# An attention and mixture-of-experts layer: each routed expert's weights loaded in two halves, the second one tile behind the first

## The reference

```python
logits = flat @ router_w.T
scores = jnp.sqrt(jax.nn.softplus(logits))
_, idx = jax.lax.top_k(scores + expert_bias, K)          # K = 4
topv = jnp.take_along_axis(scores, idx, axis=1)
topv = topv / (topv.sum(axis=-1, keepdims=True) + 1e-20)
probs = jnp.zeros((T, E), flat.dtype).at[jnp.arange(T)[:, None], idx].set(topv)

def body(acc, xs):
    wg, wu, wd, p = xs
    return (acc + p[:, None] * _clamped_swiglu(flat, wg, wu, wd), None)
out, _ = jax.lax.scan(body, jnp.zeros_like(flat), (gate_w, up_w, down_w, probs.T))
out = out + _clamped_swiglu(flat, shared_gate_w, shared_up_w, shared_down_w)
```

## Time and profile before

| | us |
|---|---|
| median of 3 runs | 1499.61 |
| lowest, highest | 1496.22, 1509.61 |
| the profiled execution's own time | 1504.55 |
| its span on the core | 1502.6 |

### The profile page before, as it was taken

How to read it: one execution, slowest core, us unless ns; L and a number is a source line. 1 busy time by engine, 2 the same in 40 slices (tenths; PEclk the granted TensorE clock), 3 DMA queues, 4 the chain that set the end, 5 groups by cost and what they waited for, 6 DMA issues and landing times.

```text
span 1502.6 us, 28760 instructions
## 1 busy us (share of the span) xinstructions
PE 1300.7 (87%) x7954; PEld 647.3 (43%) x7955; DVE 989.5 (66%) x1847; ACT 794.2 (53%) x1022; POOL 871.5 (58%) x883
## 2 busy tenths in 40 slices
PE   7999678887888888888887588799999899999998
PEld 3333234443444444444444344344444444444443
DVE  7555699999999999999999257433333233323333
ACT  2222499998999999999999431122222121212221
POOL 3111388889899999999999403434343443444441
PEclk9999699999999999999999689999999999999999
DMA  9664178776676776676777365465666666665432
GB/s 267 159 157 98 32 130 142 135 141 133 140 146 142 141 144 133 139 141 139 145 137 131 103 247 183 158 180 112 190 186 188 190 151 162 158 179 123 83 57 72
DMA packets 387509, 217.60 MB, mean 145 GB/s; under 512 B 348279, under 2 KB 348407, under 8 KB 383234
## 3 DMA queue, kind: packets, MB, share of 16 engines
q1 hardware_dynamic: 369586, 182.34, 50.0%
q0 software_dynamic: 17872, 34.64, 12.5%
HBM read 104.47 MB, written 37.49 MB: 94 GB/s over the span
## 4 chain that ended last, share of the span: by engine, by line
PE 29%; issue 21%; DMA 17%; DVE 14%; POOL 10%; ACT 5%; SPq 2%; DVEq 2%; POOLq 1%; ACTq 0%
PE psS L773 14%; DMA out_y<-mem 11%; POOL mem L649 6%; DVE mem L565 4%; DVE mem L581 4%; PE psS L781 4%; DMA mem<-mem 3%; ACT mem L526 2%; PE psS L1608 2%; PE psS L446 2%; DMA mem<-xn_dram,mem 2%; POOL mem L638 1%; DVEq L1192 1%; PE psP L765 1%; PE psP L1589 1%
## 5 line engine op out<-in xcount | busy, mean ns | idle before, releaser
L526 ACT ACTIVATE mem<-mem 128x2048 uint8<-128x2048 f32 x256 | 535.3, 2093 | 46.0 <-POOL mem L638 41.2
L649 POOL TENSOR_SCALAR mem<-mem 128x2048 bf16<-128x2048 uint8 x256 | 486.2, 1899 | 28.3 <-DMA mem<-mem 9.2
L446 PE MATMUL psS<-mem 128*128 128x512 bf16 x1024 | 312.6, 388 | 97.8 <-DVE mem L565 49.1
L773 PE MATMUL psS<-mem 128*128 (+1 forms) x752 | 356.9, 617 | 0.1
L581 DVE TENSOR_SCALAR_CACHE_REDUCE mem<-psS,mem 128x1024 f32<-128x1024 f32 x256 | 328.1, 1282 | 0.9 <-PE psS L446 0.9
L565 DVE TENSOR_SCALAR_CACHE_REDUCE mem<-psS 128x1024 f32<-128x1024 f32 x256 | 313.0, 1223 | 15.0 <-PE psS L446 11.4
L807 DVE TENSOR_SCALAR mem<-psS 128x512 f32<-128x512 f32 x94 | 65.2, 693 | 344.3 <-PE psS L773 341.3
L1170 POOL DMA_INDIRECT out_y<-mem x78 | 124.0, 1589 | 189.3 <-DMA out_y<-mem 153.0
L801 ACT ACTIVATE mem<-mem 128x256 f32<-128x256 f32 x94 | 39.4, 419 | 360.8 <-DVE mem L807 360.8
L773 PEld LDWEIGHTS psS<-mem 128*128 128x128 f32 x752 | 139.9, 196 | 151.7 <-issue 148.8
L781 PE MATMUL psS<-mem 128*128 (+1 forms) x376 | 177.1, 592 | 1.0 <-ACT mem L795 1.0
(11 more groups left out here) (213 smaller groups left out, 1192.8 us busy)
## 6 DMA issues: line engine op xcount, KB each, us to landing
mem<-in_moe_w SPq DMA_DIRECT2D x33, 1536.0 KB, 8.1
xn_dram<-mem SPq DMA_DIRECT2D x33, 256.0 KB, 2.4
mem<-in_x SPq DMA_DIRECT2D x32, 256.0 KB, 3.1
mem<-xn_dram SPq DMA_DIRECT2D x32, 256.0 KB, 3.0
out_y<-mem SPq DMA_DIRECT2D x32, 256.0 KB, 2.3
mem<-mem SPq DMA_TRANSPOSE x288, 3.1
mem<-in_ctx_in SPq DMA_DIRECT2D x16, 256.0 KB, 3.2
mem<-out_y SPq DMA_DIRECT2D x16, 256.0 KB, 4.1
```

Source lines behind the costliest of these rows:

```text
L446: last = nc.tensor.matmul(psS[c][:, k * D:(k + 1) * D], qT[pm][:, hm, :], kT[:, hm, c * HALF + k * D:c * HALF + (k + 1) * D], start=True, ...
L526: nc.scalar.activation(p8[slot], S[slot], ACT.Exp, bias=NB[:, slot:slot + 1], scale=sq[p][:, h:h + 1], accum_out=Z[p][:, h:h + 1]).then_in ...
L649: nc.gpsimd.tensor_scalar(pb[slot], pT[slot].bitcast(U8).rearrange("p (j q b) -> p j b q", b=2, q=P), 1.0, 0.0, ALU.mult, ALU.add).then_in ...
L773: last = nc.tensor.matmul(bankG[o], xT[o if xo is None else xo][:, c, :], w(c * 2 * I, 2 * I), start=(c == 0), stop=(c == DC - 1))
```

## The change

The load of an expert becomes two DMAs. Each takes half of the words of every partition row: 6 KB from each of 128 rows instead of 12 KB, 768 KB in all instead of 1,536. Where the place is free from the start (experts 0 to 7), the two are issued one behind the other. In the ring (experts 8 to 31), the first half is issued when the old load was, and the second when PE has finished one more down product, so one tile later. `expert_in` counts to 32 instead of 16 per use of a place.

```diff
+        def load_expert(sp, e, s, piece):
+            words = slice(piece * EW // 2, (piece + 1) * EW // 2)
+            sp.dma_start(ring[:, s * EW + words.start:s * EW + words.stop], moe_w[e, :, words]).then_inc(expert_in[s], 16)
+
...
                 if k < FREE_RING:
-                    sp.dma_start(ring[:, k * EW:(k + 1) * EW], moe_w[k, :, :]).then_inc(expert_in[k], 16)
+                    for piece in range(2):
+                        load_expert(sp, k, k, piece)
...
             for s in range(FREE_RING, RING):
-                sp.dma_start(ring[:, s * EW:(s + 1) * EW], moe_w[s, :, :]).then_inc(expert_in[s], 16)
+                for piece in range(2):
+                    load_expert(sp, s, s, piece)
             for s in range(RING):
-                sp.wait_ge(expert_in[s], 16)
+                sp.wait_ge(expert_in[s], 32)
                 sp.sem_inc(expert_there, 1)
...
                 sp.wait_ge(down_mm, done)
                 apart(sp, done)
-                sp.dma_start(ring[:, s * EW:(s + 1) * EW], moe_w[e, :, :]).then_inc(expert_in[s], 16)
+                load_expert(sp, e, s, 0)
                 if e > RING:
-                    sp.wait_ge(expert_in[(e - 1) % RING], 16 * ((e - 1) // RING + 1))
+                    sp.wait_ge(expert_in[(e - 1) % RING], 32 * ((e - 1) // RING + 1))
                     sp.sem_inc(expert_there, 1)
-            sp.wait_ge(expert_in[(E - 1) % RING], 16 * ((E - 1) // RING + 1))
+                sp.wait_ge(down_mm, done + 1)
+                apart(sp, done)
+                load_expert(sp, e, s, 1)
+            sp.wait_ge(expert_in[(E - 1) % RING], 32 * ((E - 1) // RING + 1))
             sp.sem_inc(expert_there, 1)
```

## The result

| | before | changed |
|---|---|---|
| median of the runs, us | 1503.37 (4 runs, 1496.22 to 1509.61) | 1485.62 (4 runs, 1479.81 to 1488.41) |
| profiled execution's own time | 1504.55 | 1486.25 |
| its span | 1502.6 | 1484.3 |

The ratio is 0.9885, with a 95% interval of 0.9841 to 0.9928: 1.2% faster. The forecast was 1512 with a range of 1487 to 1519. Ratios here leave out the one run that lies over 1.5% above the fastest of its kernel, in the slower state that the chip at times shows; it is one of `count_between`.

A forecast was written before the change was run, and what follows sets the result against it. PE looked saturated, with half a microsecond a tile lost to a register-load loop, then to lagging scatters. Holding the loop's pace (+9.5) less one slip (-2) gave +7.5 on 1504.55: 1512 us, range 1487 to 1519.

The forecast's parts named there:

- the slow step: Routed stage, first stretch: 6.49 us a tile instead of 5.98; held for 72 tiles it adds 9.5 us.
- What still throws it out: Ring loads of single-tile experts: two halves together act as a whole load, one slip expected, -2 us.
- The excess wait shrinks by 0.23 us a tile: After a slip, some 0.6 us of scatter wait shrinks by 5.98 - 5.75 a tile, gone in three tiles or so.
- stops: Tiles 22 to 57: scatter lag exceeds four buffers and everybody waits; 18.6 us in the kernel before.
- the first rival: Also Rival 1: lag still comes but halves remove its stops, 1486 us; chance 0.18 for 1475 to 1490, 0.10 for 1490 to 1498.
- The loop through the register load: First stretch: scatter, DVE's delayed expert-number load, copies, next scatter; a 6.56 us cycle that needs no weight load.
- 5.98 us is what PE's own work costs: Routed tiles 57 to 77 come every 5.98 us, taken as the cost of PE's own work per tile.
- A single half-load in step: First stretch: a half lands after 4.7 us, meets the scatter's issue for 0.6 us, and should not use up the slack.
- The cover of the weights: Ring: the later second half is needed seven experts later, some 17 tiles or 100 us, so it costs nothing.
- The eight more issues ahead: Before the routed stage: eight extra DMA issues on SP, taken as 0, at most 2.7 us.
- Rival 3: Stretch with loads: each half disturbs the scatter like a whole load, 2.0 us each, +50 us, 1554; chance 0.04.

The follow-up runs named there:

- count_between: The changed kernel with SP reading the next expert's count between the two halves of an expert: 1487.1 us against 1499.9, ratio 0.9903.
- whole_tile_later: The kernel before with every ring load whole but issued one tile later: 1499.2 us against 1503.3, ratio 0.9989.
- both_at_once: The changed kernel with both halves of a ring load issued together when the place is free: 1499.4 us against 1503.3, ratio 0.9991.
- early_halves: The changed kernel with halves only for experts 0 to 7, ring loads whole and undelayed: 1498.0 us against 1501.1, ratio 0.9982.

## Why the prediction was wrong, point by point

- **The kernel would hold the slow step for all 72 tiles (+9.5 us; its own 467.3 - 457.9 gives 9.4): wrong, and the step of the prediction that failed is the one under "What still throws it out" (-2 us).** I had taken a pair of half-loads for a whole load again, and given it one slip in seven. The pair is not one load: SP's register load stands between its issues, the second comes 1.1 us ahead of the scatter, and the next scatter is stretched to 9.06 us, not 7.05. With that register load moved it was 6.90 us, and the step was left at tile 25 instead of 13. From tile 5 to 77 I had 467.3 - 2 = 465.3 us; measured were 436.8, so the term would have had to be -30.5 instead of -2.
- **"The excess wait shrinks by 0.23 us a tile": failed too, in the same step.** With half-loads about, pairs among them, the scatters come every 6.05 us on average, so the lag stays. Had I laid the halves' own disturbance beside PE's 5.98 once the kernel is out of step, I could have seen that it need not come back.
- **What the change gains outside the slow step: priced at nothing, and it is the larger part.** A kernel in step has no stops, so the forecast had no term for them. Out of step, the stops of whole loads are gone: 16.6 of the 21.1 us, near the 18.6 of the first rival. `whole_tile_later` and `both_at_once` leave the step as early, keep the stops, and gain little if anything (ratios 0.9989 and 0.9991).
- **The loop through the register load: right.** The kernel without ring loads runs in it for nearly all tiles, 1509.0 where I had 1512 for a kernel in step, and moving the register load removes it. But "5.98 us is what PE's own work costs" was read wrong: the fast register load is in it, and without it a tile takes 5.88 to 5.92.
- **A single half-load in step does no harm: right.** `count_between` ran 20 tiles in step, and none of the 13 scatters there with one half-load ahead of it was followed by more than 6.7 us. The changed kernel's halves land 4.4 us after the issue from 1007 to 1081 us, where 4.7 had been estimated:

```profile
mem<-in_moe_w SPq DMA_DIRECT2D x7, 768.0 KB, 4.4
```

- **The cover of the weights: right.** No wait of PE for a weight load shows in the changed kernel's waits.
- **The eight more issues ahead (0 to 2.7 us): open.** The first routed gate came 3.8 us later in this trace, but among the kernels with the same early part it lies anywhere between 972.6 and 981.2 us, so one trace can't tell. `early_halves` was not slower than before.
- **Rival 1: right in kind, and its 1486 to the microsecond is luck.** The stops went (16.6 us, priced at 18.6), but the step was also left earlier (4.9 us, not in its sum), the last tiles took 0.4 more, and the two ends of the span added 2.8. A chance of 0.18 for 1475 to 1490 was too low. What spoke for it was in the profile: the kernel before had left the same loop after 17 tiles in its own trace, and a step that one transfer can end should not have been given 78 tiles.
- **Rival 3: false.** One half issued about a microsecond ahead disturbs a lagging scatter by some 0.4 us, not by 2.0; two together come to as much as 2.6.

## What to carry to other kernels

When a kernel has two modes of nearly the same pace, ask of a change not only what it costs in the mode of the trace but which mode it leaves the kernel in, and for how long; a transfer that is free in one phase can be what ends it. Spreading a prefetch in time paid here because a serial chain of small transfers, each waiting for the last to land, shares its DMA engines (1485.6 with the halves a tile apart, 1499.4 with both at once); look whether one burst fits into the gap of such a chain. And put a register load on an engine's queue ahead of a wait that is there anyway: behind the gate it cost 39 us here, where whole weight loads, with it out of the way, cost 25 (1494.7 against 1469.8).

## What was not expected of the hardware

A load of one word from SBUF into a register of DVE takes 301 to 306 ns in the fast stretches (median 306). All such loads of over 0.6 us in the routed stage of the traces here started 2.0 to 3.5 us after the issue of a scatter; they took up to 1.15 us. In the kernel without ring loads they ended 3.3 us after that issue in the median, so no weight load is needed for it. What holds them (the scatter's descriptors, its first packets) stays open.

The Trainium skill (DMA: Bandwidth & Descriptors, Latency and other measured facts) gives `tensor_load` a floor of about 600 ns. The 301 to 306 ns here are below it, so the measurement decides.

Leaving out 36 MB of transfers made the kernel slower by 0.45% (1509.0 against 1503.3), since it kept the kernel in its slow step.
